# Products of zeros on TensorE ahead of three kinds of waits, in a Perceiver block of two layers

## What is computed

```python
x = x + _L0_xattn_ref(_layernorm(x), ctx_512, ...)   # A: causal cross attention, 16 heads
x = x + _L0_attn_ref(_layernorm(x), ...)             # B: self attention with rotary positions
x = x + _L0_ffn_ref(_layernorm(x), ...)              # C: two passes of 8 gated experts
x = x + _L1_xattn_ref(_layernorm(x), ctx_512, ...)   # D: latent cross attention over 1601 keys
x = x + _L1_attn_ref(_layernorm(x), ...)             # E: a Mamba-2 mixer, 32 heads
x = x + _L1_ffn_ref(_layernorm(x), ...)              # F: 8 experts of SwiGLU, two chosen per token

def _layernorm(x, axis=-1, eps=1e-05):
    m = jnp.mean(x, axis=axis, keepdims=True)
    v = jnp.var(x, axis=axis, keepdims=True)
    return (x - m) / jnp.sqrt(v + eps)
```

## Time and profile before

| | us |
|---|---|
| median of 3 runs | 1502.19 |
| lowest and highest of them | 1499.42, 1504.19 |
| profiled execution, its own time | 1504.73 |
| its span, first to last instruction | 1501.8 |
| TensorE matmul busy | 1382.3 |
| VectorE busy | 1058.1 |
| GpSimd busy | 702.0 |
| ScalarE busy | 634.8 |

### The profile page before, as it was taken

The page is one execution under the profiler, slowest core; times in us unless marked ns, Lnnn a source line. Parts: engine busy times, 40 slices in busy tenths (PEclk is TensorE's granted clock), DMA queues, the critical chain, the costliest instruction groups (busy, mean ns, idle before and its releaser), DMA issues.

```text
span 1501.8 us, 23786 instructions
## 1 busy us (share of the span) xinstructions
PE 1382.3 (92%) x8654; PEld 1151.0 (77%) x8655; DVE 1058.1 (70%) x1575; ACT 634.8 (42%) x1331; POOL 702.0 (47%) x468
## 2 busy tenths in 40 slices
PE   6787799999999999799999999999899888979998
PEld 4565578867877787589899999999778676756886
DVE  5648476668657888677777777777547999946555
ACT  3332253344332323366656566666325545432000
POOL 3334147767847677314413412500364665524663
PEclk9998799999999999999999999999999999999999
DMA  3111113322332322000000000100131222212321
GB/s 137 44 42 58 42 49 92 97 79 84 92 128 85 96 80 80 31 23 2 25 24 1 25 24 1 52 1 1 51 103 57 71 61 67 66 43 74 96 89 69
DMA packets 31475, 87.92 MB, mean 59 GB/s; under 512 B 3472, under 2 KB 3600, under 8 KB 31120
## 3 DMA queue, kind: packets, MB, share of 16 engines
q1 hardware_dynamic: 31376, 86.53, 19.0%
HBM read 85.46 MB, written 1.05 MB: 58 GB/s over the span
## 4 chain that ended last, share of the span: by engine, by line
PE 67%; DVE 16%; issue 8%; ACT 8%; POOL 1%; DMA 0%; ACTq 0%; DVEq 0%; POOLq 0%
PE psum L808 20%; PE psum L809 19%; PE psum L810 19%; DVE conv_acc L2518 3%; PE psum L1286 3%; DVE part_max L2402 3%; ACT expo L1792 2%; ACT expo L1797 2%; ACT expo_t L1804 2%; PE psum L831 1%; PE psum L839 1%; DVE sq_sum L2631 1%; DVE expo_t L1998 1%; DVE psum L2589 1%; PE psum L917 1%
## 5 line engine op out<-in xcount | busy, mean ns | idle before, releaser
L635 POOL TENSOR_SCALAR wpair<-landing 128x1024 fp32r<-128x1024 f32 (+3 forms) x120 | 113.4, 945 | 427.3 <-PE psum L810 320.1
L638 POOL TENSOR_TENSOR wpair<-landing,wpair 128x1024 fp32r<-128x1024 f32 (+3 forms) x120 | 254.9, 2125 | 10.0
L808 PE MATMUL psum<-xn,wpair 128*128 128x512 f32 (+1 forms) x548 | 214.7, 392 | 5.3 <-POOL wpair L638 4.1
L809 PE MATMUL psum<-xn,wpair 128*128 128x512 f32 (+1 forms) x548 | 210.2, 384 | 0.0
L810 PE MATMUL psum<-xn,wpair 128*128 128x512 f32 (+1 forms) x548 | 209.3, 382 | 0.0
L1998 DVE TENSOR_TENSOR expo_t<-psum,expo_t 128x512 fp32r<-128x512 f32 (+1 forms) x224 | 143.6, 651 | 79.2 <-ACT expo_t L1804 77.3
L1804 ACT CAST expo_t<-psum 128x512 fp32r<-128x512 f32 (+1 forms) x224 | 124.2, 564 | 128.6 <-PE psum L1286 127.8
L808 PE MATMUL psum<-expo_t,kv_pair 128*128 128x256 f32 (+1 forms) x416 | 133.6, 321 | 4.1 <-DVE expo_t L1998 4.1
L1286 PE MATMUL psum<-const,expo 128*128 128x128 f32 (+1 forms) x832 | 128.3, 274 | 5.0 <-DVE kv_t L1998 4.3
L2402 DVE TENSOR_REDUCE part_max<-psum 128x1 f32<-128x804 f32 x128 | 122.9, 987 | 13.6 <-PE psum L810 11.7
L808 PEld LDWEIGHTS psum<-xn,wpair 128*128 128x128 f32 x548 | 104.7, 191 | 30.2 <-POOL wpair L638 4.8
(11 more groups left out here) (308 smaller groups left out, 3408.6 us busy)
## 6 DMA issues: line engine op xcount, KB each, us to landing
landing<-in_weights SPq DMA_DIRECT2D x71, 512.0 KB, 3.6
landing<-in_weights SPq DMA_DIRECT2D x97, 256.0 KB, 2.6
kv<-in_ctx SPq DMA_DIRECT2D x8, 832.0 KB, 4.4
landing<-in_weights SPq DMA_DIRECT2D x16, 384.0 KB, 3.1
landing<-in_weights SPq DMA_DIRECT2D x15, 320.0 KB, 2.9
rope_k<-in_rope_k SPq DMA_DIRECT2D x1, 1664.0 KB, 7.9
const<-in_constants SPq DMA_DIRECT2D x1, 1184.0 KB, 8.7
x<-in_x SPq DMA_DIRECT2D x4, 256.0 KB, 4.2
```

The costliest lines, as they stand in the source:

```text
L635: pool.tensor_scalar(wpair[:, slot, 0, 0:width], landing[:, slot, 0:width], 1.0, 1.0, ALU.mult, ALU.mult).then_inc(chunk_high, 1)
L638: pool.tensor_tensor(wpair[:, slot, 1, 0:width], landing[:, slot, 0:width], wpair[:, slot, 0, 0:width].bitcast(F32), ALU.subtract).then_in ...
L808: pe.matmul(out, w(0), act(0), start=start, stop=False)
L809: pe.matmul(out, w(0), act(1), start=False, stop=False)
```

## The change

Three places on TensorE get products of bf16 zeros, 128 x 128 by 128 x 512, that start and stop a sum of their own in a bank that is not in use: six ahead of each half's sums of squares in the norms k = 1 to 5, eight ahead of the wait for `ctx_low` of head 0, and seven ahead of the last down products, these behind a new wait until ScalarE has read bank 0. The banks' later users start their sums anew, so no result changes. No other engine's program is touched.

```diff
+            def keep_going(k_bank, products):
+
+                for _ in range(products):
+                    pe.matmul(bank(k_bank), zero_b[:, 0:P], zero_b[:, :], start=True, stop=True)
+
...
                 for half in range(2):
+                    if k:
+                        keep_going(LN_BANKS[k][1 + half], 6)
                     for pair in range(2):
                         square_sums(k, half, pair)
...
-                def value_latents(h, slot, buffer):
+                def value_latents(h, slot, buffer, waiting=0):
                     chunk_ready(D3B + h)
+                    keep_going(2, waiting)
                     pe.wait_ge(ctx_low, h + 1)
...
-                value_latents(0, D3B % 2, 0).then_inc(chunk_used, 1)
+                value_latents(0, D3B % 2, 0, 8).then_inc(chunk_used, 1)
...
                         expert_f(2 * i + j + 2, FB + 7 + 6 * i + 3 * j, (FB + 1 + j) % 2)
+                pe.wait_ge(silu_done, 2 * 3 * NE)
+                keep_going(0, 7)
                 down(FB + 25, (FB + 25) % 2, 3 * NE - 1, True)
```

## The result

| | before | after |
|---|---|---|
| median of 7 runs each, alternating, us | 1499.72 | 1494.21 |
| lowest and highest, us | 1496.63, 1504.19 | 1489.51, 1499.31 |
| profiled execution, us | 1504.73 | 1495.74 |
| ratio of the times, 95% interval | 1 | 0.995 [0.993, 0.997] |

The change makes the kernel faster by 0.5%, 5.5 us by the medians. The forecast was 1500.0 from a median of 1502.19, a gain of 2.2 us.

What follows compares the result with a forecast made beforehand. TensorE, busy 92% of the span with some 84 us at half clock, was the bound. Gains of 4.45 us from the profiled 1504.73 gave 1500.3, 2.3 from the median 1502.19 gave 1499.9; forecast 1500.0 us, range 1495.8 to 1503.8.

Steps and rivals of the forecast that it cites:

- The zeros fit the gaps.: TensorE's gaps: six zeros take 1.40 us of 1.60 and 1.69, eight 1.87 of 2.54, seven 1.64 of 2.39, at no cost.
- The new wait costs nothing.: Ahead of the last down products, which wait for VectorE's low halves at 1489.4 anyway; cost nothing.
- The filled gaps give 1.5 + 1.4 + 1.55 = 4.45 us in the profiled execution, 2.3 in a typical one.: Half-clock stretches avoided at sixth norm, first latent product and last down products: 1.5, 1.4 and 1.55 us.
- The reduction from 4.45 to 2.3: Another execution loses 2/3 x (1.4 + 1.55) = 2.0 us at the two long gaps, some 0.3 in the norms.
- The rule cited from the Trainium skill on longer waits: Waits that bring the clock down are longer than the three filled, so the change gives nothing: 1502.2 us.
- It removes nothing. ... No DMA and no other queue is touched. The sum is one of covers and of falls avoided.: Whole change: it adds 75 products and one wait; gains come only from covered gaps and avoided drops to half clock.
- More than the sum: Rival: two of five norms lose 1.5 us in a typical run, plus both long gaps; 6 us, 1496.2; chance 0.19.
- The falls only move.: Rival: shifted work meets other unfilled gaps, three new drops to half clock undo the sum; 1502.2 us; chance 0.10.
- The zeros get in the way: Rival: zeros at half clock end after the awaited data, twice a norm; loss up to 11.5 us, 1513.7; chance 0.07.
- The zeros don't hold the clock: Rival: zero products may not count as activity for TensorE's clock, so no change, 1502.2 us; chance 0.06.

Runs made afterwards that it cites:

- wide_late: The changed kernel without the zeros of the second to fourth norm, which stand ahead of D's loop; median 1497.89 us, ratio 0.999 [0.9972, 1.0008].
- whole_moved: The changed kernel plus 92 products 8 columns wide, in two long waits ahead of D's loop; median 1498.79 us, ratio 0.9988 [0.9973, 1.0002].
- pad_early: The changed kernel with only the 36 products of the second to fourth norm, each 8 columns wide; median 1496.69 us, ratio 0.9977.
- narrow: The changed kernel with all 75 zero products 8 columns wide in place of 512; median 1495.67 us, ratio 0.9976.
- norms_only: The changed kernel without the eight and seven zeros and the new wait, leaving the five norms' zeros; median 1491.85 us, ratio 0.996.
- more_heads: The changed kernel with wide zeros at five more places, and ahead of heads' scores and turned probabilities in A and B; median 1501.68 us, ratio 1.0007.
- pad_24: The changed kernel with only the products of the second and third norm, 8 columns wide, 48 instructions ahead of D's loop; one run, 1508.12 us.
- latent_only: The changed kernel with only the eight zeros ahead of the first latent product; median 1497.66 us, ratio 0.9979.
- pad_12: The changed kernel with only the 12 products of the second norm, 8 columns wide, 24 instructions ahead of D's loop; one run, 1502.27 us.
- pad_96: The changed kernel with only sixteen products, 8 columns wide, in each gap of the second to fourth norm; one run, 1500.11 us.

## Why the prediction went wrong

**The zeros fit the gaps.** Right. Six records end before the squares arrive; the sums follow with 0.24 us of idle time or none. From the first squares to the next product the sixth norm now takes 5.21 us, as the third did before and does still.

**The new wait costs nothing.** Right: the last down products begin behind VectorE's low halves, with 0.71 us idle behind the zeros.

**The filled gaps give 1.5 + 1.4 + 1.55 = 4.45 us in the profiled execution, 2.3 in a typical one.** Right. The profiled pair shows 1.52 + 1.47 + 1.55 = 4.54. In the runs wide_late, which has all of these and the old layout, gains 2.0 ± 0.9, and whole_moved 2.0 ± 0.8. The reduction from 4.45 to 2.3, made by counting how many like gaps are followed by a fall, was the better half of the prediction. The fourteen traces bear it out:

| place | traces without the wide zeros, with a fall there | traces with them, with a fall there |
|---|---|---|
| sixth norm | 8, 2 | 6, 0 |
| first latent product | 8, 5 | 6, 0 |
| last down products | 8, 5 | 6, 0 |

Over the eight without, the falls cost 0.4, 1.0 and 0.9 us on average at the three places, 2.3 together. The rule cited from the Trainium skill on longer waits, by which the change would give nothing, doesn't hold here: these falls followed waits of 1.44 to 2.38 us, and are gone where the waits are filled.

**"It removes nothing. ... No DMA and no other queue is touched. The sum is one of covers and of falls avoided."** This is the step that failed. The change touches TensorE's own program, and with it the loads that bring it. It moved the body of D's loop by 72 instructions, so that the two turns back take 0.2 us in place of 3.3 to 3.9. It is worth 4.5 ± 1.0 us (pad_early), 4.0 ± 0.5 (narrow), or 4.7 ± 1.5 (whole_moved against after, the other way round). The prediction had nothing for it. With the 2.3 of the forecast that makes 6.3 to 7.0, and the measured gain by means is 6.7 ± 1.3. The rows stood in the trace of before: waits of 1.94 us at 748.86 and 1.64 at 857.37, and 71 loads on the page. I had read the waits that the change touches and not the others, and these two carry ScalarE's name.

**"More than the sum", 1496.2.** It came nearest in size, for a reason that the traces speak against, so this nearness is luck. Norms whose falls the trace didn't show were to give 3 us. But narrow and pad_early, whose norms are not filled, keep 4.0 and 4.5 us of norms_only's 6.9, and of the 43 norms that stand without wide zeros in the nine traces that have such, the second to the sixth, only two have a fall over their sums, both the sixth.

**"The falls only move."** Partly: stage B takes 1.03 us more, with a clock of 0.89 in 90 to 120 us where before had 1.00 (narrow, without work in the gaps, has 0.89 there too), and two falls behind the turns went with their waits. The three new falls that would undo the sum are not there; the half-clock time went from 74 to 66.1 us.

**"The zeros get in the way"** did not happen in this change. It did in more_heads, in the form that the prediction described: zeros at the half clock with nothing to cover them. **"The zeros don't hold the clock"** is refuted by the table above, no fall in 18 filled places against 12 in 24 unfilled ones. narrow alone, with 3.37 us at the latent product in place of 2.38, would not do, as three of the eight traces without wide zeros have 2.35 there.

What stays open: in the seven traces with loads at the turns, pad_24 apart, the two eighths are on average 5.5 us longer than in the six without, and the runs show 4.0 to 4.7. How often a fall follows a turn's wait is not settled by one trace a kernel. norms_only is 3.0 ± 1.1 us faster than narrow by the means, more than the falls of the sixth norm account for. And the profiled execution of whole_moved has the slow operations of stage E (below) and that of after has not; how often the other runs of each kernel have them isn't recorded, so some of the 4.7 ± 1.5 may be theirs. The waits, the branches and the eighths don't depend on that.

## What to carry to other kernels

An edit that only adds instructions can move a loop behind it in its engine's program, and a loop whose body just fits or just doesn't pays for it at each turn: compare the count of instruction loads on the two pages first, and look at the first wait behind each turn, whoever is named as its releaser. Filling a wait of 1.4 to 2.4 us with zeros pays 1.5 us where a fall of the clock would have followed, and then only if the zeros stand ahead of the wait, end before it does, and run at the full clock. To test what an edit does by its place alone, put in the same number of instructions with 8 columns each.

## What the runs showed of the hardware

A branch back in TensorE's program took 0.21 to 0.24 us where its target was held, and 3.3 to 3.9 us where it was loaded: the load began 0.9 to 1.5 us after the branch and took 0.9 to 1.5 us. The array hid about half of that with work already queued.

In these profiles a wait for program is credited to another engine at the turn (ScalarE, 1.94 us in before), and shows as "issue" in the three kernels where it stands further in (2.19 us in pad_24).

In eight of fourteen traces (latent_only, narrow, wide_late, more_heads, whole_moved, pad_12, pad_24, pad_96) the same two operations of VectorE in stage E take 2 to 3 us more than in the others. The timeline of before and of wide_late:

```profile
1267.40 1.29 DVE L2555 TENSOR_TENSOR decay_in<-const,a_pair 128x512 fp32r<-128x512 f32 x2
```

```profile
1265.83 4.29 DVE L2565 TENSOR_TENSOR decay_in<-const,a_pair 128x512 fp32r<-128x512 f32 x2
```

Stage E is some 4 us longer with it, 206.1 to 207.7 us from the fifth norm's squares to the sixth's in place of 201.9 to 202.2. What differs is GpSimd. Its operations of splitting a chunk of weights in before, behind VectorE's two, and in wide_late, over them:

```profile
1268.75 1.04 POOL L635 TENSOR_SCALAR wpair<-landing 128x1024 fp32r<-128x1024 f32 x1 [8.02 <-PE psum L810]
1269.88 2.36 POOL L638 TENSOR_TENSOR wpair<-landing,wpair 128x1024 fp32r<-128x1024 f32 x1
```

```profile
1265.43 1.39 POOL L635 TENSOR_SCALAR wpair<-landing 128x1024 fp32r<-128x1024 f32 x1 [6.26 <-PE psum L810]
1266.90 2.67 POOL L638 TENSOR_TENSOR wpair<-landing,wpair 128x1024 fp32r<-128x1024 f32 x1
```

It holds throughout: of this operation of VectorE the fourteen traces have 224 records. 188 took 0.7 us, and none of them overlaps a TENSOR_TENSOR of GpSimd; 36 took 1.5 to 2.9 us, and every one does. This shows that the two come together, not which holds up which; no run moved GpSimd's work. Its split starts once TensorE has released the chunk before (the brackets), and so comes earlier or later. Six of the eight kernels with loads at the turns have the overlap and two of the six without, which is no clear link in one trace a kernel.
